# Head projections of an attention and feed-forward block on one Trainium2 core: weights laid out by the host, output buffers doubled, a stored product no longer made from a turned matrix

## The reference, cut to what matters

```python
x = x + attn(layernorm(x)); x = x + ffn(layernorm(x))      # x: 1 x 2048 x 512, float32
# attn, 16 heads, scale 128 ** -0.5
q_lat = x @ Wq_down                      # 512 -> 256
q = [heads(q_lat @ Wq_up), rope(heads(q_lat @ Wq_rope))]   # 64 + 64 per head
kv_lat = x @ Wkv_down                    # 512 -> 128
k = [heads(kv_lat @ Wk_up), rope(heads(x @ Wk_rope))]
v = heads(kv_lat @ Wv_up)                # 128 per head
out = softmax(causal(q @ k.T * scale)) @ v
return concat(out) @ Wo                  # 2048 -> 512
# ffn: three weight matrices rounded to -1, 0, 1 times their mean absolute value
return (silu(x @ wu.T) * (x @ wg.T)) @ wd.T
```

## Time and profile before

| | us |
|---|---|
| three runs, median | 2084.41 (2083.89 to 2088.01) |
| profiled execution, span of core 0 | 2084.8 |
| `latents`, to the first instruction of the next stage | 71.3 |
| `heads_inputs`, from SP's first weight load (73.57) to its end (354.79) | 281.2 |
| busy in the span: PE, DVE, ACT, POOL | 1950.1, 1339.8, 1058.0, 526.0 |
| mean granted clock of TensorE | 0.976 |

### The profile page before, as it was taken

How to read it: one execution, slowest core, us unless ns; L and a number is a source line. 1 busy time by engine, 2 the same in 40 slices (tenths; PEclk the granted TensorE clock), 3 DMA queues, 4 the chain that set the end, 5 groups by cost and what they waited for, 6 DMA issues and landing times. The chain is left out here.

```text
span 2084.8 us, 32094 instructions
## 1 busy us (share of the span) xinstructions
PE 1950.1 (94%) x11562; PEld 1666.1 (80%) x11562; DVE 1339.8 (64%) x2574; ACT 1058.0 (51%) x2533; POOL 526.0 (25%) x333
## 2 busy tenths in 40 slices
PE   6888885899999999999999999999999979999999
PEld 5766664788888898888888888888888868787877
DVE  5455453678778778778687687777777773333333
ACT  3233332666567566566566576666666652222222
POOL 6234343623223321321331322312422100000000
PEclk9998988899999999999999999999999999999999
DMA  3597988622020220220210202202202030000000
GB/s 109 146 231 204 227 203 214 188 62 48 30 61 18 60 61 1 77 61 1 77 44 19 77 11 51 77 1 61 61 17 61 1 122 1 20 0 20 0 20 20
DMA packets 67558, 144.12 MB, mean 69 GB/s; under 512 B 6880, under 2 KB 23648, under 8 KB 63328
## 3 DMA queue, kind: packets, MB, share of 16 engines
q1 hardware_dynamic: 67424, 142.31, 25.8%
HBM read 94.04 MB, written 48.23 MB: 68 GB/s over the span
## 5 line engine op out<-in xcount | busy, mean ns | idle before, releaser
L998 ACT CAST turned_hi<-ps_turn 128x512 fp32r<-128x512 f32 (+1 forms) x576 | 314.8, 567 | 403.0 <-PE ps_turn L1165 403.0
L1064 DVE TENSOR_TENSOR turned_lo<-ps_turn,turned_hi 128x512 fp32r<-128x512 f32 (+1 forms) x576 | 370.3, 659 | 156.0 <-ACT turned_hi L998 156.0
L968 ACT ACTIVATE probs<-ps_scores,bias 128x512 f32<-128x512 f32 (+3 forms) x642 | 402.4, 636 | 19.3 <-DVE bias L1057 11.9
L1051 DVE TENSOR_REDUCE negmax<-ps_scores 128x1 f32<-128x512 f32 (+2 forms) x576 | 342.3, 616 | 6.1 <-PE ps_scores L1131 5.5
L1165 PE MATMUL ps_turn<-ident,probs 128*128 128x128 f32 x2176 | 320.1, 276 | 0.6
L1131 PE MATMUL ps_scores<-k_hi,q_hi 128*128 128x512 f32 (+2 forms) x642 | 261.2, 407 | 35.0 <-issue 22.6
L1165 PEld LDWEIGHTS ps_turn<-ident,probs 128*128 128x128 f32 x2176 | 247.8, 141 | 24.2 <-ACT probs L968 2.3
L1142 PE MATMUL ps_o<-turned_hi,kv_hi 128*128 128x256 f32 x1152 | 254.2, 302 | 3.0 <-DVEq L1063 3.0
L1131 PE MATMUL ps_scores<-k_hi,q_lo 128*128 128x512 f32 (+2 forms) x642 | 237.5, 370 | 0.0
L1131 PE MATMUL ps_scores<-k_lo,q_hi 128*128 128x512 f32 (+2 forms) x642 | 237.5, 370 | 0.0
L1142 PE MATMUL ps_o<-turned_hi,kv_lo 128*128 128x256 f32 x1152 | 231.9, 283 | 0.0
(11 more groups left out here) (159 smaller groups left out, 3450.9 us busy)
## 6 DMA issues: line engine op xcount, KB each, us to landing
rotT<-rot_out SPq DMA_DIRECT2D x64, 256.0 KB, 3.5
plainT<-plain_out SPq DMA_DIRECT2D x64, 256.0 KB, 5.1
k_raw<-plainT SPq DMA_DIRECT2D x16, 512.0 KB, 5.6
k_raw<-rotT SPq DMA_DIRECT2D x32, 256.0 KB, 6.4
q_raw<-plainT SPq DMA_DIRECT2D x16, 512.0 KB, 8.4
q_raw<-rotT SPq DMA_DIRECT2D x32, 256.0 KB, 9.2
all_signs<-signs SPq DMA_DIRECT2D x24, 256.0 KB, 4.8
signs_in<-all_signs SPq DMA_DIRECT2D x12, 512.0 KB, 9.7
```

Source lines behind the costliest of these rows:

```text
L968: nc.scalar.activation(probs[:, u % 2, t, first_key:first_key + keys], ps_scores[:, n % RING, 0:keys], ACT.Exp, bias=bias_of(u, t), accum_ ...
L998: nc.scalar.copy(turned_part(0, n, u, s), turned_psum(n, u, s)).then_inc(turned_hi_ready, 1)
L1051: nc.vector.tensor_reduce(put, ps_scores[:, n % RING, 0:tile[p][1]], AX_X, ALU.max, negate=True).then_inc(bias_ready if whole else max_don ...
L1064: nc.vector.tensor_tensor(turned_part(1, n, u, s), turned_psum(n, u, s), turned_part(0, n, u, s).bitcast(F32), ALU.subtract).then_inc(turn ...
```

## The change

- `pair_w` is a new input that the host makes: for each pair and each of 128 partitions its nine blocks of 128 columns side by side (4608 bytes), rotary halves already in their order. One transfer loads it, one instruction on ACT and one on POOL split it. This splitting stands at c = 2 and no longer at c = 1.
- `vo_w` is a new input: for each head Wv, already turned by the host, beside Wo (640 columns, 2560 bytes to a partition). It is loaded, split and multiplied one head at a time, at c = 1 and c = 3 (`VO_AT`), into one buffer `vo_raw`. PE turns nothing here. Each head's result is stored alone (256 KB).
- `rot_out` and `plain_out` have two buffers for each group, chosen by c % 2, each with a semaphore of its own.
- In `latents` each latent product stands before the turning of the same i, and AHEAD is 1.

The core of the diff:

```diff
 def load_pair_weights(sp, hbm, pair_w, pair, loaded):
-    cols = bass.ds(pair * P, P)
-    for name, s0, k in (("Wq_rope", ROT_Q, KQ), ("Wk_rope", ROT_K, KD), ("Wq_up", PLAIN_Q, KQ), ("Wk_up", PLAIN_K, 1)):
-        sp.dma_start(pair_w["raw"][:, s0:s0 + k, :],
-                     hbm[name].rearrange("(k p) n -> p k n", p=P)[:, :, cols]).then_inc(loaded, 16)
+    sp.dma_start(pair_w["raw"][:], hbm["pair_w"][bass.ds(pair, 1), :, :].rearrange("a p (k n) -> p (a k) n", n=P)
+                 ).then_inc(loaded, 16)
...
-    AHEAD = 2
+    AHEAD = 1
...
                     if 1 <= c <= NC and i < NL:
+                        latent(c - 1, i)
                     if c < NC:
...
+                        turn(TC * c + i)
...
-        rot_out = sb("rot_out", [P, 2, CH])
-        plain_out = sb("plain_out", [P, 2, CH])
+        rot_out = sb("rot_out", [P, 2, 2, CH])
+        plain_out = sb("plain_out", [P, 2, 2, CH])
...
+        VO_AT = (1, 3)
+
+        def load_vo(sp, head):
+            sp.dma_start(vo_raw[:], hbm["vo_w"][bass.ds(head, 1), :, :]).then_inc(vo_loaded, 16)
...
+                        if c in VO_AT:
+                            h = VO_AT.index(c)
+                            head = 2 * pair + h
+                            sp.wait_ge(wvo_copied, 2 * j + h + 1)
+                            sp.dma_start(hbm["wvo"].rearrange("(h p) n -> h p n", p=P)[bass.ds(head, 1), :, :],
+                                         wvo_out[:]).then_inc(wvo_stored, 16)
+                            load_vo(sp, (head + 1) % H if h == 0 else 2 * following)
...
+                        if c in VO_AT:
+                            act.wait_ge(vo_loaded, 16)
+                            act.sem_inc(vo_loaded, -16)
+                            nc.scalar.copy(vo[0][:], vo_raw[:]).then_inc(vo_hi_ready, 1)
                         for g in range(2):
                             act.wait_ge(plain_ready, PER_PAIR * j + 2 * c + g + 1)
-                            act.wait_ge(plain_stored[g], 16)
+                            act.wait_ge(plain_stored[2 * g + c % 2], 16)
...
-                        if c == 1:
-                            act.wait_ge(w_loaded, 16 * NW * (j + 1))
-                            act.sem_inc(wv_landed, 1)
+                        if c == 2:
+                            act.wait_ge(w_loaded, 16 * (j + 1))
                             split_hi(1 - j)
-                            nc.scalar.copy(wo[0][:], wo_raw[:]).then_inc(wo_hi_ready, 1)
...
+                        if c in VO_AT:
+                            h = VO_AT.index(c)
+                            dve.wait_ge(vo_hi_ready, 2 * j + h + 1)
+                            nc.vector.tensor_tensor(vo[1][:], vo_raw[:], vo[0][:].bitcast(F32), ALU.subtract
+                                                    ).then_inc(vo_lo_ready, 1)
...
+                        if c in VO_AT:
+                            pe.wait_ge(vo_lo_ready, 2 * j + h + 1)
+                            for n, (a, b) in enumerate(parts(0, 1)):
+                                last = nc.tensor.matmul(ps[:, WVO0, :], vo[a][:, 0:P], vo[b][:, P:P + D],
+                                                        start=(n == 0), stop=(n == 2))
+                            last.then_inc(wvo_ready, 1)
```

More of the change, by code:

```diff
@@ L213, in _ @@
                                                 ALU.subtract).then_inc(xt_lo_ready, 1)
[L214 to L221, removed]
+                if c + AHEAD < NC:
+                    chunk_stats(c + AHEAD)
                 if c >= 2:
@@ L261, in _ @@
                 for i in range(TC):
+                    if 1 <= c <= NC and i < NL:
+                        act.wait_ge(lat_ready, NL * (c - 1) + i + 1)
+                        nc.scalar.activation(lat(0, i, c - 1), ps[:, LAT0 + i, :], ACT.Copy,
+                                             scale=lat_scale(i)).then_inc(lat_hi_ready, 1)
                     if c < NC:
@@ L276, in _, with turn, latent @@
                                    ps[:, KV0, :].rearrange("p (t n) -> p t n", t=TC)).then_inc(kv_hi_copied, 1)
-                if c + AHEAD < NC:
-                    root(c + AHEAD)
                 if c == SPLIT_AT:
-                    act.wait_ge(pair_loaded, 16 * PAIR_LOADS)
-                    for n, (raw, hi, _lo) in enumerate(pair_views(pair_w, 0)):
-                        last = nc.scalar.copy(hi, raw)
-                    last.then_inc(pair_hi_ready, 1)
+                    act.wait_ge(pair_loaded, 16)
+                    nc.scalar.copy(pair_w["split"][0][0][:], pair_w["raw"][:]).then_inc(pair_hi_ready, 1)
         @block.tensor
         def _(pe):
+            def turn(t):
+                pe.wait_ge(xn_ready, t + 1)
+                if t >= 2:
+                    pe.wait_ge(xt_lo_ready, t - 1)
+                for k in range(KD):
+                    last = nc.tensor.transpose(ps[:, t % 2, k * P:(k + 1) * P],
+                                               x[:, t, k * P:(k + 1) * P], ident[:, :])
+                last.then_inc(xt_ready, 1)
+            def latent(c, i):
+                if i == 0:
+                    pe.wait_ge(xt_lo_ready, TC * (c + 1))
+                    if c == 0:
+                        pe.wait_ge(wlat_lo_ready, 1)
+                if c > 0:
+                    pe.wait_ge(lat_lo_ready, NL * (c - 1) + i + 1)
+                n = 0
+                for k in range(KD):
+                    for a, b in parts(0, 1):
+                        last = nc.tensor.matmul(ps[:, LAT0 + i, :], w[a][:, k, i * P:(i + 1) * P],
+                                                xT[b][:, k, c * CH:(c + 1) * CH],
+                                                start=(n == 0), stop=(n == 3 * KD - 1))
+                        n += 1
+                last.then_inc(lat_ready, 1)
             pe.wait_ge(ident_loaded, 16)
@@ L1546, in program @@
             for n in ("rot", "plain"):
-                keep[f"{n}_stored"] = [c1.enter_context(nc.semaphore(f"{n}_stored{g}")) for g in range(2)]
+                keep[f"{n}_stored"] = [c1.enter_context(nc.semaphore(f"{n}_stored{b}")) for b in range(4)]
             keep["wvo_stored"] = c1.enter_context(nc.semaphore("wvo_stored"))
@@ L1572, in constants, with by_pair, slices, by_head @@
     return {"ident": np.eye(P, dtype=np.float32), "mask": mask, "cos": cos, "sin": sin}
-NAMES = ("x", "Wq_down", "Wq_up", "Wq_rope", "Wkv_down", "Wk_up", "Wk_rope", "Wv_up", "Wo", "W_up", "W_gate", "W_down")
+def by_pair(wq_rope, wk_rope, wq_up, wk_up):
+    def slices(w, rotated):
+        cols = w.reshape(-1, P, PAIRS, 2, 2, HALF)
+        if rotated:
+            cols = cols.transpose(0, 1, 2, 4, 3, 5)
+        return cols.reshape(-1, P, PAIRS, P)
+    every = [slices(wq_rope, True), slices(wk_rope, True), slices(wq_up, False), slices(wk_up, False)]
+    return np.ascontiguousarray(np.concatenate(every).transpose(2, 1, 0, 3).reshape(PAIRS, P, NSL * P))
+def by_head(wv, wo):
+    return np.ascontiguousarray(np.concatenate([wv.reshape(KVR, H, HD).transpose(1, 2, 0), wo.reshape(H, HD, D)], axis=2))
+NAMES = ("x", "Wq_down", "Wkv_down", "W_up", "W_gate", "W_down")
 def kernel(**inputs):
```

162 lines of the change are left out of this document (49 added, 113 removed).

## The result

The changed kernel takes 2097.76 us (median of 4 runs, 2095.92 to 2098.53), the one before, on the same chip, 2084.97 (4 runs, 2083.89 to 2088.01): a ratio of 1.0055, interval 1.0043 to 1.0068. The forecast was 2054 us (2028 to 2074).

The account below looks back on a forecast made before the run. Bound taken: a burst at each pair's start that one output buffer cannot cover. Seven pairs x (35.15 - 31.1) = 28.4 us, first pair 2.8, first stage +0.7: 2084.8 - 30.5, so 2054 us, range 2028 to 2074.

Parts of the forecast that it names:

- What bounds the kernel: Heads stage, 35.15 us a pair: a burst at the pair's start that one output buffer cannot cover; DMA then idles.
- Doubled output buffers, 7.7 us a pair: Start of a pair: PE's 5.48 us stall and the half clock behind it go, 34.2 to 26.5 us.
- the ring: Once per pair: waits through the landings of W_gate and vo_raw and the work between them, setting 31.1 us a pair.
- The step that failed most: Pair-weight split moved to c = 2: POOL's part costs nothing, ACT's part takes 1.15 us within the ring.
- Host layout and no turning of Wv: Weight loads: 0.4 us less DMA a pair; PE's two dropped turnings, about 0.3 us each, counted as nothing.
- First stage, +0.7: Latents stage: first product 2.9 us sooner, later chunks +0.6, +1.8 and +1.2, so the last chunk starts 0.7 us later.
- Rival 3: Moved split and single vo_raw slow the pair if landings reach 7.0 us or more; up to 2106 us; chance 0.08.
- Rival 4: Buffers were no bound, PE's wait only moves: 2084 us; chance 0.07, shared with Rival 1 to the end.
- Rival 1: Stores pace the pair at 33 us, 2068 us, or 35.1, no change; chance 0.18 partly, 0.07 shared with Rival 4.
- Rival 2: Transfers get faster under even load, pair falls toward PE's 26.2 us plus 0.7: 2020 to 2032 us; chance 0.20.

Follow-up runs that it names:

- a5: Changed kernel with one output buffer per group again for rot_out and plain_out: 2101.32 us, 1.0065.
- a7: a6 with all output buffers single: 2077.28 us, 0.9941.
- a6: Changed kernel with pair split at c = 1, early vo_raw load, old first stage, two FFN chunk buffers loaded earlier, single plain-K output buffer: 2077.76 us, 0.9948.
- c3: c1 with single output buffers: 2069.64 us, 0.9904.
- c1: b1 with vo_hi and vo_lo made one chunk ahead of their products: 2065.86 us, 0.9888.
- a2: Changed kernel with the next vo_raw issued ahead of the chunk's stores and TensorE's Wv Wo released later by the same signal: 2093.44 us, 1.0037.
- a8: Changed kernel with two FFN chunk buffers, loaded ahead of the chunk's stores, and a single plain-K output buffer: 2101.19 us, 1.0063.
- a1: Changed kernel with the pair's weights split at c = 1 again on ACT and POOL: 2078.35 us, 0.9961.
- b2: Changed kernel with vo_lo behind the chunk's multiplications on DVE: 2085.46 us, 0.9994.
- b1: Changed kernel with pair split at c = 1, old first stage, vo_lo behind the multiplications, next vo_raw issued behind the rotary stores: 2080.96 us, 0.9971.
- c2: c1 with the pair's weights split at c = 2, as in the changed kernel: 2062.23 us, 0.987.
- a3: Changed kernel with the first stage in its former order (turning first, AHEAD = 2): 2099.6 us, 1.0053.

## Why the prediction was wrong

- **What bounds the kernel.** The reading that a single output buffer holds ACT and POOL was right as a row of the kernel before and wrong as the cause of its 35 us a pair: ACT's wait fell by half, POOL's for a store went, and nothing was gained. In a5, which has the single buffers back, POOL waits for VectorE all the same (its second addition 1.1 us behind the first).
- **Doubled output buffers, 7.7 us a pair.** Mis-sized: by the medians, single buffers cost 2 us in the whole kernel (a5), nothing (a7 against a6) or 3 us (c3 against c1), at most half a microsecond a pair. TensorE's waits for ACT were gone in a5 and a7 with single buffers, so it was another part of the change, or the new waits ahead of it, that took them away. Which of them was not tested; that the change spreads the burst of loads at the pair's start over the pair is one candidate.
- **What is late next, the ring.** From the fourth pair's landing of W_gate to the fifth's, the links measure 13.9 us to the issue of `vo_raw` (predicted 11.7), 5.8 (5.2), 9.4 (9.0), 5.9 (4.9): 35.0 us against 30.8. Of the first one's 2.2 us, 1.9 are `vo_lo`, 2.71 instead of 0.83. This agreement does not prove the ring. Stretches laid end to end from one landing to the same landing a pair later add up to the pair, whatever sets it. Taking its landings out (a2, a6, a8) gained nothing in the pairs, though each of these edits added a wait elsewhere. What did pay was shortening the stretch between the landings, where one engine's wait passes through `vo_hi` and `vo_lo` to all others (a1, b2, and c1 against b1).
- **The step that failed most.** "POOL splits the pair's weights at c = 2 ... so this costs nothing", with 1.15 us for ACT's part. It cost 20 us (a1), 2.5 us a pair. Two things stand behind it, 1.14 us on ACT ahead of `vo_hi` and 1.89 us more for `vo_lo`, which meets POOL's subtraction; their shares were not separated. I had looked only at whether POOL's result is late for TensorE, and not at who stands behind ACT's part or runs beside POOL's.
- **What is still open.** Without the moved split the kernel is at 2078 us (a1), by the ratios still 22 above the forecast. At the stage's end its profile is 20 us behind the forecast's sum: 2 at the first load, 3 in the first pair, 9.5 in pairs 2 to 7 (32.69 us and not 31.1), 6 in the last with its wait for the useless load. What sets the 32.69 us was not found; the versions with the early split come down to 31.66 and 31.37 (c1, c2).
- **Host layout and no turning of Wv.** Counted as 0.4 us a pair, which set nothing in the sum, and as nothing. No run takes these parts alone. That c3 and a7 gain with single output buffers leaves room for more than that.
- **First stage, +0.7.** Near in size: latent products start at 19.70, 34.27, 48.41 and 60.80 us (predicted 19.8, 34.2, 47.45, 60.1), the next stage 1.4 us later. Undoing it gains nothing (a3).
- **Missing.** The wait at the stage's end for the useless `vo_raw`: +4.4 us on the last pair, one third of the loss (a2 gave 3.9 us of it back), and readable from the diff alone: a load moved behind the last store, and a wait for it behind the loop.
- **Rivals.** Rival 3 had the right sign and place, but the wrong price: it wanted landings of 7 us and more (`vo_raw` landed in 6.0, W_gate in 5.9), and it had a chance of 0.08. Rival 4, that the wait only moves, describes the middle of the stage (35.0 and 35.2 us) and shared a chance of 0.07. Rival 1 is ruled out as a bound at 35 us: c2 moves the same bytes at 240 GB/s, with 31.37 us a pair. Rival 2 did not come.

## What to carry to other kernels

Removing the longest wait is worth only what the next link in the same chain leaves; before pricing it, follow the in-order queues and ask for each engine what stands behind its new wait. A high/low split that crosses two engines couples their queues: put both halves a step ahead of their use and behind the work that others wait for. When a block is moved in one queue, look at what then runs beside it on the other engines, and when a prefetch is moved to the loop's end, at who waits for the last one.

## What the runs showed of the hardware

VectorE's subtraction with both operands in SBUF (128 x 640) takes 0.82 us alone and 2.71 us where it starts 0.6 us behind GpSimd's subtraction of 2.61 us (207.85 and 207.27 us, rows above). GpSimd's record ends at 209.88 us, VectorE's at 210.56, 0.68 us later, so most of VectorE's 0.82 us of work was done after GpSimd had ended. It goes the other way round too. In c2_early_split_c2 VectorE starts first, keeps its 0.83 us, and GpSimd's addition takes 1.86 us in place of 1.30:

```profile
207.18 0.83 DVE L543 TENSOR_TENSOR vo_lo<-vo_raw,vo_hi 128x640 fp32r<-128x640 f32 x1 [0.25 <-DVE by_sin L533]
207.29 1.86 POOL L497 TENSOR_TENSOR rot_out<-by_cos,by_sin 128x512 f32<-128x512 f32 x1 [1.12 <-POOLq L496]
```

The multiplications, which read one operand from PSUM, keep their 0.69 us beside GpSimd (c2 again):

```profile
218.32 0.69 DVE L530 TENSOR_TENSOR by_cos<-ps_proj,cos 128x512 f32<-128x512 f32 x1 [0.33 <-DVE by_sin L533]
218.35 1.29 POOL L497 TENSOR_TENSOR rot_out<-by_cos,by_sin 128x512 f32<-128x512 f32 x1 [3.17 <-POOLq L496]
```

The Trainium skill ("SBUF — State Buffer", Who interferes with whom) says that a VectorE instruction with two SBUF inputs and a GpSimd instruction that reads SBUF exclude each other, and that the one issued first decides who waits. These rows agree on both counts, and the price here is 1.89 us of VectorE's time a pair.
